# GpSimd's sums over a tile's heads, with and without a wait for the masks of a later tile

## The reference, cut to what matters

```python
sim = jnp.einsum('pbthn,hkpn->pbthk', q, keys)
scores_xy, idx_xy = jax.lax.top_k(sim, K)
...
scores, pk = jax.lax.top_k(all_scores, K)
indices = jnp.take_along_axis(all_idx, pk, axis=-1)
de = down_embed[indices]
ue = up_embed[indices]
w = jax.nn.silu(jnp.einsum('btd,bthkd->bthk', hidden_states, de) * jax.nn.softmax(scores, axis=-1))
experts_states = jnp.einsum('bthk,bthkd->btd', w, ue)
dense = jnp.einsum('bti,di->btd', jax.nn.silu(jnp.einsum('btd,id->bti', hidden_states, W_up)), W_down)
return dense + experts_states
```

## Time and profile before

| | |
|---|---|
| median of 3 runs | 1268.8 us (1267.45 to 1272.27) |
| the profiled execution | 1258.83 us, its span 1257.0 us |
| busiest engines over the span | PE 83%, DVE 62%, ACT 52%, POOL 35% |
| the 16 tiles of this part | about 374 to 717 us from the span's start |
| granted TensorE clock in that stretch | 0.98 of full speed (2.4 GHz) |

### The profile page before, as it was taken

How to read it: one execution, slowest core, us unless ns; L and a number is a source line. 1 busy time by engine, 2 the same in 40 slices (tenths; PEclk the granted TensorE clock), 3 DMA queues, 4 the chain that set the end, 5 groups by cost and what they waited for, 6 DMA issues and landing times.

```text
span 1257.0 us, 16614 instructions
## 1 busy us (share of the span) xinstructions
PE 1048.3 (83%) x5420; PEld 651.6 (52%) x5420; DVE 778.1 (62%) x1940; ACT 659.1 (52%) x870; POOL 443.4 (35%) x350
## 2 busy tenths in 40 slices
PE   5696989989766799899999878999998894499991
PEld 3342343433244687787778653433433332388881
DVE  2664767678259777877876225676767663344443
ACT  3043555656545686767777621566655463255550
POOL 1327676655320434334344510020322323222220
PEclk9577998999968999999999995999998887699996
DMA  8835856857799600000000056455453416222226
GB/s 235 209 99 181 253 160 172 260 185 247 168 236 232 133 1 1 1 1 1 1 1 1 1 134 127 121 138 163 110 162 92 104 51 277 89 71 72 74 64 201
DMA packets 77801, 151.68 MB, mean 121 GB/s; under 512 B 8234, under 2 KB 48300, under 8 KB 76182
## 3 DMA queue, kind: packets, MB, share of 16 engines
q1 hardware_dynamic: 67446, 107.72, 33.3%
q0 software_dynamic: 9168, 42.12, 10.1%
q10 hardware_dynamic: 1104, 0.79, 0.2%
HBM read 73.88 MB, written 76.25 MB: 119 GB/s over the span
## 4 chain that ended last, share of the span: by engine, by line
PE 55%; DVE 20%; ACT 7%; issue 7%; POOL 5%; DMA 4%; SPq 1%; ACTq 0%; DVEq 0%; POOLq 0%
PE ps L1135 14%; PE ps L1053 7%; PE ps L1022 7%; DVE negmax L1358 6%; PE ps L1001 6%; PE ps L1036 4%; PE ps L1010 3%; PE ps L1235 3%; PE ps L1198 3%; PE ps L1212 2%; DMA sq<-m_sb 2%; PE ps L1062 1%; PE ps L1309 1%; DVE moe_w L1613 1%; POOL pt L626 1%
## 5 line engine op out<-in xcount | busy, mean ns | idle before, releaser
L1358 DVE TENSOR_REDUCE negmax<-ps 128x1 f32<-128x512 f32 x512 | 321.2, 682 | 74.0 <-PE ps L1022 70.9
L795 ACT ACTIVATE pt<-ps 128x1024 f32<-128x1024 f32 x256 | 255.8, 1025 | 157.0 <-PE ps L1036 150.3
L1022 PE MATMUL ps<-sk,sq 56*128 56x512 f32 x512 | 175.0, 478 | 48.3 <-DVE negmax L1358 21.2
L1053 PE MATMUL ps<-pt,v_aug 128*32 128x512 f32 x1024 | 146.9, 648 | 20.8 <-POOL pt L626 19.9
L1022 PEld LDWEIGHTS ps<-sk,sq 56*128 56x128 f32 x512 | 77.9, 207 | 116.6 <-DVE negmax L1358 73.7
L1036 PE MATMUL ps<-sq,sk 57*128 57x512 f32 x512 | 131.2, 501 | 3.2 <-DMA sq<-m_sb 1.8
L626 POOL TENSOR_TENSOR pt<-pt,near 128x512 f32<-128x512 f32 x64 | 81.5, 1274 | 114.4 <-ACT pt L795 114.3
L1036 PEld LDWEIGHTS ps<-sq,sk 57*128 57x128 f32 x512 | 51.8, 196 | 101.1 <-issue 65.0
L708 POOL TENSOR_TENSOR x_tok<-x_tok,on 128x256 f32<-128x256 f32 x16 | 11.6, 725 | 234.0 <-DVE on L1378 234.0
L730 POOL DMA_INDIRECT expert_out<-yo,dest x39 | 38.1, 976 | 116.0 <-ACT yo L941 85.7
L666 POOL TENSOR_TENSOR w_first<-w_first,moe_w 128x1024 f32<-128x1024 f32 x16 | 38.1, 2379 | 108.1 <-DVE pt L1605 107.3
(11 more groups left out here) (253 smaller groups left out, 1957.3 us busy)
## 6 DMA issues: line engine op xcount, KB each, us to landing
expert_rows<-zero SPq DMA_DIRECT2D x3, 5586.0 KB, 57.8
qk_rows<-hl SPq DMA_DIRECT2D x32, 512.0 KB
expert_weights_split<-wst POOLq DMA_DIRECT2D x8, 2048.0 KB, 8.2
sq<-qk_rows SPq DMA_DIRECT2D x64, 192.0 KB, 4.7
sk<-qk_rows SPq DMA_DIRECT2D x64, 192.0 KB, 5.5
qk_rows<-hl SPq DMA_DIRECT2D x32, 256.0 KB
moe_w<-in_w POOLq DMA_DIRECT2D x16, 512.0 KB, 10.2
wexp<-expert_weights_split POOLq DMA_DIRECT2D x16, 512.0 KB, 4.9
```

The lines of the kernel that those rows point to most:

```text
L795: act.activation(pt[:, 4 * (U % 2) + 2 * half:4 * (U % 2) + 2 * half + 2, :], ps[:, 2 + 2 * half:4 + 2 * half, :], ACT.Exp, scale=(BIAS, S ...
L1022: pe.matmul(ps[:, jbank(job), :], sq[r, pair, t * P:(t + 1) * P], sk[r, pair, :], start=True, stop=True).then_inc(s_job, 1)
L1053: ins = pe.matmul(ps[32 * j:32 * j + 32, OBANK, :], v_aug[:, b % 2, c, HG * g + j, :], pt[:, 4 * (U % 2) + j, :], start=(c == 0), stop=(c ...
L1358: dve.tensor_reduce(negmax[:, n % 2, col:col + 1], src, AX, ALU.max, negate=True).then_inc(s_jd, 1)
```

## The change

The wait for the mask goes, and in the code the sums of tile s - 1 stand behind the clamped pairs of tile s:

```diff
             pool.wait_ge(s_wl, 1)
-            for s in range(NTL + 2):
-                if s < NTL:
-                    pool.wait_ge(s_pm, RH * s + 1)
-                if s >= 2:
-                    add_heads(s - 2)
+            for s in range(NTL + 1):
                 if s < NTL:
                     clamped_pairs(s)
+                if s >= 1:
+                    add_heads(s - 1)
```

## The result

The changed kernel took 1282.5 us (median of 4; 1276.93 to 1285.08) against 1268.1 us: a ratio of 1.0142 with a 95% interval of 1.0097 to 1.0186, 1.4% or 18 us slower by this ratio (the medians differ by 14.4), and slower by more than 0.5% at either end. The forecast was 1285.7, with 1270 to 1290. Run once more on another chip it was 1.0087 (1.0059 to 1.0115). The difference is 16.8 us.

The account below looks back on a forecast made before the run. No engine fills the span (TensorE nearest, 83%), so waits count; VectorE bounds odd tiles. Five pairs at 3.3 us (16.4) and 0.5 for tile 2 make +16.9 on the median 1268.8: 1285.7 us, range 1270 to 1290.

Parts of the forecast that it names:

- The place and the mechanism: Earlier GpSimd sums hold top8 in even tiles and add_pair in odd ones; a sum between add_pair's products, chance 0.45.
- D: VectorE's delay in an odd tile from held add_pair products: 4.3 us taken; a pair gains below 1.03.
- Even tiles: In tile 10 sums hold L1582 by 1.7 and L1592 by 0.8 us, 2.5 together; cost nothing.
- The cover: VectorE's idle room in even tiles takes up the delay of top8; it is 1.4 us wide.
- The price of a pair: Each odd-even pair from tiles 5, 7, 9, 11 and 13 costs D - 1.03 = 3.3 us; five make 16.4.
- the 1.03 that I took: What a pair gets back from D: TensorE's shift is D - 0.5, and ScalarE regains 0.54 before L813.
- the sum of 16.9: Total cost in us: five pairs, 16.4, and tile 2, estimated at 0.5; tile 15 absorbed.
- With nothing lost about 3 us: Gain without collisions: about 0.5 us per odd tile, five of them with tile 2 about 3 us.
- only these 0.54 come back: Of the removed waits in an odd tile, only ScalarE's 0.54 us wait for turn_sim is regained.
- VectorE keeping its turn: Rival: VectorE runs both L1635 before the third sum, D = 2.35; +7.1, 1275.9 us; chance 0.30.
- L1635 not held: Rival: add_pair's products pass, L1582 is held, D = 1.8; +4.5, 1273.3 us; chance 0.08.
- no change: Rival: silu and norms8, not the mask, hold the sums, so nothing changes; 1268.8 us; chance 0.10.

Follow-up runs that it names:

- e1: The changed kernel with the wait for the mask put back ahead of sums that run into an odd tile; ratio 0.9986 to the kernel before.
- e5: The changed kernel with ten unused TensorE products ahead of the logits of head 2 in odd tiles 5 to 13; ratio 1.0041 to the kernel before.
- e10: The changed kernel again, unchanged, on the same chip as a rerun of the kernel before; ratio 1.0087 to the kernel before.
- e3: The changed kernel with only each tile's first sum early, the second and third waiting for the mask as before; ratio 0.9888 to the kernel before.
- e8: The same kernel as e3, run for a second profile and more times; ratio 0.9866 to the kernel before.
- e11: The same kernel as e3, on the chip of e9 and e10; ratio 0.9855 to the kernel before.
- e2: The changed kernel with the wait for the mask put back ahead of sums that run into an even tile; ratio 1.0097 to the kernel before.
- e6: The changed kernel with all three sums waiting for the end of the next tile's top8; ratio 1.0040 to the kernel before.
- e4: The changed kernel with each sum replaced by three memsets of the same buffer, experts' contribution left out; ratio 0.9901 to the kernel before.
- e9: The kernel before again, unchanged, for a second profile on the chip of e10 and e11; ratio 0.9995, stage 346.3 us.

## Why the prediction was right, step by step

- **The place and the mechanism: right.** Removing the wait let the sums meet top8 and add_pair. Add_pair's two products are held, each by a sum, with GpSimd between the two. I had given this 0.45; all twelve products show it. D was forecast 4.3 and is 5.09 - 0.88 = 4.2 in tile 11.
- **Even tiles: right in the outcome, wrong in one row.** L1582 was forecast to be held 1.7 and is held 1.7 (2.14 less 0.42). Behind it I expected L1592 to meet the third sum; the conversion L1590 in front of it did. The cover held (e1), though the idle time of mask(s, 2) fell from 3.71 to 1.5.
- **The price of a pair: 3.3 forecast, 2.9 without a fall of the clock (e5).** Of the difference 0.1 is D; some 0.3 more came back behind the mask than the 1.03 that I took. Part of that is ScalarE: its copy of turn_sim (L813, after L811) follows the logits of head 2 by 10.77 us in tile 11 of the changed kernel and by 11.44 in tile 9 of before, 0.67 less where I took 0.54. The rest I did not put down to one wait.
- **TensorE's clock: missed.** I took it as unchanged. Behind the new idle stretch of 3.4 us ahead of the logits it is halved in three of five tiles, in both profiles of the changed kernel (e10: tiles 5, 9 and 11, in tile 5 for twice as long), 1.6 us for a single fall, 5 us in the stage; e5, with the stretch filled, has none. That the sum of 16.9 met a measured 16.8 of the stage is luck, since this and other terms are set against each other: 14.4 of held products (five times 2.88) and 4.9 of clock, less the fall that before's tile 5 had (1.4) and less 1.1 in the rest (1.0 more in tiles 0 to 3, where I had put 0.5, and 2.1 less in the last two).
- **"With nothing lost about 3 us": too small.** The pairs gain 0.7 (0.5 forecast), but tile 2 gains 3.5, not 0.5, and the odd tiles lose their falls of the clock. By the ratios of e3, e8 and e11 it is 14 to 18 us. What failed is "only these 0.54 come back": it followed the chain at full clock, and did not ask what TensorE's idle stretch, which the gains shorten, does to its clock. The falls of the stage that went are shown (one or four from tile 5 on, 1.4 each, and one in tile 2, 1.6); the stage is 5 to 13 us shorter by the profiles, so some us of the 14 to 18 lie outside it and stay open.
- **The rivals.** VectorE keeping its turn, L1635 not held, and no change are all excluded by the two products of 2.57 in each tile. No run had a D between 0 and 4.2, so the point from which a pair gains, D = 1.03, is untested.
- **The median.** 16.9 was set on 1268.8 for 1285.7; measured 1282.5, 14.4 above the median of the runs beside it, and 9.6 above on another chip. One profile of before is one draw: its stage differed by 4 us between two, and the program behind the stage by 7 (by 14 between the two of the changed kernel). So it is in part luck, too, that the median came within 3.2 us of the forecast.

## What to carry to other kernels

Ask of a wait that looks idle what it keeps apart. Here GpSimd sat idle 9 to 13 us before its sums, and the wait put them beside masks, which they don't disturb (only norms8's small product was held); split by sum, the wait could go where it hurt (head 2, which ScalarE waits for) and stay where it protected (heads 0 and 1, kept off add_pair and top8): that version is 1.1 to 1.5% faster than before, and on one chip 1241.3 us against the changed kernel's 1268.6, 2.1%. When a stall on another engine leaves TensorE idle for two or three us, price the clock behind it too, and look at it in more than one execution.

## What the runs showed of the hardware

- A VectorE product of two SBUF tensors that meets a GpSimd sum (2.38 us, two inputs in SBUF) is held to about the sum's end, whatever its own length: 2.57 instead of 0.48, 2.14 instead of 0.42, 1.75 instead of 0.18. Masks with one input in PSUM were not: two took 2.47 beside a sum and 2.48 without one, and no single mask took over 1.29 in any run.
- Between add_pair's two products, which stand on VectorE without a wait between them, GpSimd's next sum got in every time: in all six tiles of the changed kernel, and again in e2, e5 and e10.
- A VectorE instruction with one tensor in SBUF and scalars is held as well: norm1, 4.97 instead of 0.74 for two (e6), and the conversion of 32 indices, 0.79 instead of 0.16. Both are held even by GpSimd's memsets (0.63, and 1.12 for one instruction of norm1, e4); the products of add_pair and top8 beside memsets are not (0.485 and 0.43 at most).
- TensorE's granted clock halved for about 3 us (in tile 5 of e10 for twice as long) behind idle stretches of 1.7 to 3.4 us in some tiles and not in others of the same form: tile 9 and tile 11 of the changed kernel, or tile 9 of the kernel before (idle 1.69, no fall) and of e9 (1.67, a fall).
- The second layer's attention, the same instructions in all kernels, took 256.7 us at a mean granted clock of 0.90 (e10) and 270.9 at 0.86 (the changed kernel's first profile).
